# A cross-attention and gated feed-forward layer: queries, keys and values projected turned, their stacks built by way of a scratch in device memory, keys and values by plain fp32 matmuls

## The chip, the core and the metric

The kernel runs on one core of a Trainium2 chip. The metric is the device time of one execution in microseconds (us). One profiled execution of the kernel before is read here; its matrix engine is called PE, its weight loads PEld, the vector engine DVE, the scalar engine ACT, GpSimd POOL and the sync engine SP.

## What is computed

```python
x = x + tanh(g_xattn) * xattn(layernorm(x), ctx, ctx)   # x, ctx: 8 batches x 128 tokens x 512
x = x + tanh(g_ffn)   * ffn(layernorm(x))
# xattn: Q = q Wq + bq (32 heads of 16), K = c Wk + bk, V = c Wv + bv (8 heads of 16, 4 query heads share one)
#        w = softmax(Q K^T / 4); y = w V; return y Wo + bo
# ffn:   h = silu(x w1^T) * (x w3^T); return h w2^T     (512 -> 1792 -> 512; weights come scaled per 128x128 block)
```

All of it is float32, and the result has to be near float32.

## The kernel before, in words

**Products.** A product of near float32 accuracy is made of three fast matmuls in a reduced float32 format (fp32r) on a high and a low part of each side: high by high, high by low, low by high. `three` (lines 1765 to 1769) issues them; line 1767 is the first, 1768 the second, 1769 the third. The high part is a rounding copy on ACT (names ending in `H`), the low part a subtraction on DVE or POOL (names ending in `L`).

**Stages.** A batch is 128 tokens. Eight batches go through attention one after another, overlapped by a hand-written order on each engine: every engine has a straight list of calls with semaphore waits, and it takes them strictly in that order. After the last batch, 28 chunks of the feed-forward follow, in a loop that the change leaves alone; a few matmuls of the first chunks (`g_or_u`) stand between those of the last batches.

**One batch of attention.** `normalise` makes the layer norm, `turn4` turns it with four PE transposes, `x_high` and `x_low` split it. `project` (line 1782) gives the queries with tokens on the partitions (12 matmuls of 512 columns) and `add_bias` (line 1791) adds the bias by one more matmul of 512. Keys and values come together from `project_kv` (12 matmuls of 256 columns, on the context and weights that POOL, ACT and DVE have split) and one bias matmul of 256. `q_high`, `q_low`, `k_high`, `k_low` split them into `Qtok` and `Ktok`. Then `stack_k` and `stack_q` (lines 1795 and 1801, transposes at line 1774) turn them, four transposes at a time, and `k_stacked` and `q_stacked` (lines 614 and 618, ACT) copy the result from PSUM into the stacks: `Qst` and a part of `x2HL`, 96 rows each, in which high and low parts lie under each other so that one matmul of 96 rows gives the whole product. `Qst` holds two batches, in turns; four batches of keys have a place.

`scores` (line 1807) makes the scores of a batch in four parts, into one pair of PSUM banks, and `row_max` (line 1141, DVE) reduces each before the next may be written. The negated maxima are split, turned by `turn_max` and copied by `max_rows`; `max_in` on SP then carries them by four transfers of four rows into rows 96 to 99 of `Qst`. `scores_t` (line 1818) computes the scores again, keys on the partitions, with the maximum already subtracted. `exp_full` and `exp_half` (ACT) and `weight_low` (POOL, line 340) make the weights and their low part, `values` (line 1822, lines 1827 and 1828) the sums over the values, then follow the division, the output projection, the residual and the second layer norm.

**What sets the order.** PE takes `scores(n, 0)` only after the stacks of batch n are there. The first batch has nothing in front of it: there PE waits for weights, for splits and for stacks. SP and ACT issue the transfers; each is a queue of its own, and an issue holds its engine's list for about half a microsecond.

Of the kernel before, what the change touches and what calls it, by code (L numbers as in the profile page):

```python
# [19 lines left out]
F32 = mybir.dt.float32  # L20
F32R = mybir.dt.float32r
# [22 lines left out]
TOK = HT * P  # L44
W13 = 2 * KB * P
# [9 lines left out]
KV0, Q0, O0 = 0, KB * 2 * KVD, KB * 2 * KVD + KB * DM  # L55
PW = O0 + KB * DM
QH = Q0 + KB * DM // 2
BQ, BK, BO = 0, DM, DM + 2 * KVD
BIAS1, BIAS = BO, BO + DM
NCT, NKST = 4, 4  # L60
NWARM = 14
GATE, SC = BIAS, BIAS + 2
# [3 lines left out]
def build(nc, x, ctxt, wproj, small, wff, out):  # L66
    with ExitStack() as ctx:
# [22 lines left out]
        ctH, ctL = (context.enter_context(nc.sbuf_tensor(n, [P, 2, DM], F32R)) for n in ("ctH", "ctL"))  # L90
# [27 lines left out]
        ones = sa("ones", [P, P], F32R)  # L118
        neghalf, unit = sa("neghalf", [P, 1]), sa("unit", [P, 1])
        small1 = sa("small1", [P, 32])  # L120

        Qtok = sa("Qtok", [P, PAIRS * GJ, 3, 32], F32R)
        xTH = sa("xTH", [P, DM], F32R)
        xTL = sa("xTL", [P, DM], F32R)
        xn = sa("xn", [P, DM])
        Qst = sa("Qst", [P, 2, PAIRS, GJ * P], F32R)
        Ktok = sa("Ktok", [P, PAIRS, 2, 3, 2, DH], F32R)
        st1, mv1, ve1, rs1, nb1 = (sa(n, [P, w]) for n, w in (("st1", 6), ("mv1", 2), ("ve1", 1), ("rs1", 1), ("nb1", 1)))
        st2, mv2, ve2, rs2, nb2 = (sa(n, [P, w]) for n, w in (("st2", 6), ("mv2", 2), ("ve2", 1), ("rs2", 1), ("nb2", 1)))
        setup = ctx.enter_context(ExitStack())  # L130
        browf = sa("browf", [P, BIAS1], F32, setup)
        sel = sa("sel", [P, 2, P], F32, setup)
        one2 = sa("one2", [P, P], F32, setup)
        setup.close()
        E = sa("E", [P, NE, GJ * P])
        aTL = sa("aTL", [P, DM], F32R)
        x2n = sa("x2n", [P, DM])
        brow = sa("brow", [P, BIAS1], F32R)
        rden = sa("rden", [P, HEADS])
        vres = sa("vres", [P, KVH, DH])  # L140
# [12 lines left out]
        w2L = sb("w2L", [P, 2, DM], F32R)  # L153
        hH = sb("hH", [P, 2, TOK], F32R)
        hL = sb("hL", [P, 2, TOK], F32R)

        wkv_in, wq_in, wq2_in, wo_in, bias_in, gsc_in, bo_in = (
            sem(n) for n in ("wkv_in", "wq_in", "wq2_in", "wo_in", "bias_in", "gsc_in", "bo_in"))
# [3 lines left out]
        consts, zeros, constr, browz, tanhg = (sem(n) for n in ("consts", "zeros", "constr", "browz", "tanhg"))  # L162
        wpH_ok, wpL_ok, browH_ok, brow_ok, woL_ok, tg_ok = (sem(n) for n in ("wpH_ok", "wpL_ok", "browH_ok", "brow_ok", "woL_ok", "tg_ok"))
        sel_in, bo_ok, stats1, mean1, ve1_ok, rs1_ok = (sem(n) for n in ("sel_in", "bo_ok", "stats1", "mean1", "ve1_ok", "rs1_ok"))
        nb1_ok, xn_ok, xT_ps, xTH_ok, xTL_ok, q_ps = (sem(n) for n in ("nb1_ok", "xn_ok", "xT_ps", "xTH_ok", "xTL_ok", "q_ps"))
        qtokH, qtokL, ctH_ok, ctL_ok, kv_ps, ktokH = (sem(n) for n in ("qtokH", "qtokL", "ctH_ok", "ctL_ok", "kv_ps", "ktokH"))
        ktokL, v1_ok, r1_ok, v2_ok, v3_ok, kst_ps = (sem(n) for n in ("ktokL", "v1_ok", "r1_ok", "v2_ok", "v3_ok", "kst_ps"))
        kst_ok, qst_ps, qst_ok, s_ps, max_ok, mH_ok = (sem(n) for n in ("kst_ok", "qst_ps", "qst_ok", "s_ps", "max_ok", "mH_ok"))
        mL_ok, mT_ps, mrows, mrow_in0, mrow_in1, mrow_in2 = (sem(n) for n in ("mL_ok", "mT_ps", "mrows", "mrow_in0", "mrow_in1", "mrow_in2"))
        mrow_in3, st_ps, E_ok, PH_ok, pL_ok, pv_ps = (sem(n) for n in ("mrow_in3", "st_ps", "E_ok", "PH_ok", "pL_ok", "pv_ps"))  # L170
# [3 lines left out]
        scaled, w13H_ok, w13L_ok, g_ps, u_ps, t_ok = (sem(n) for n in ("scaled", "w13H_ok", "w13L_ok", "g_ps", "u_ps", "t_ok"))  # L174
        a_ok, h_ok, hH_ok, w2H_ok, w2L_ok, hL_ok = (sem(n) for n in ("a_ok", "h_ok", "hH_ok", "w2H_ok", "w2L_ok", "hL_ok"))
        y_used = sem("y_used")
# [3 lines left out]

        def kst(n):
            s = (NBATCH - NKST + n % NKST) * P
            return x2HL[:, :, :, s:s + P]
# [14 lines left out]
        def _(sp):  # L198
            def context_in(n):
                sp.dma_start(ct[:, n % NCT, :], ctxt[n]).then_inc(ct_in[n % NCT], 16)  # L200

            def select_rows():
                sp.wait_ge(consts, 11)
                for b in range(NKST):
                    for gg in range(2):
                        sp.dma_start(r32(kst(b)[ROWS:ROWS + 4, gg, :, :]),
                                     sel[ROWS:ROWS + 4, gg, :].unsqueeze(1).broadcast_to([4, KB, P])).then_inc(sel_in, 16)

            def max_in(n, h):
                done = (mrow_in0, mrow_in1, mrow_in2, mrow_in3)[h]  # L210
                sp.dma_start(r32(Qst[ROWS:ROWS + 4, n % 2, h, :]), r32(Mrow[4 * h:4 * h + 4, :])).then_inc(done, 16)

            def weights_in(c):
                sp.dma_start(wres[:, c, :], wff[c]).then_inc(wff_in[c], 16)

# [6 lines left out]
            for b in range(1, NCT):  # L222
                context_in(b)
# [2371 lines left out]
```

## Time and profile before

| what | us |
|---|---|
| median of 3 runs | 391.84 (390.97 to 392.38) |
| the profiled execution | 391.85 |
| its span on the core | 390.1 |
| PE busy | 377.4 (97%) |
| DVE busy | 271.7 (70%) |
| ACT busy | 209.1 (54%) |
| POOL busy | 160.5 (41%) |

What lies between the span and the execution's time is 1.75 us. A matmul's record lasts longer than its share of the engine, since matmuls are pipelined: what one costs is read from the distance between two starts, not from its duration. In the views below "x4" stands for four such instructions put into one line, and "[0.88 <-DVE Qtok L1127]" says how long the engine stood idle before the line and whose work ended that.

### The profile page before, as it was taken

The numbers are of one execution on the slowest core, as the hardware profiler recorded it, in microseconds if no ns is written. First come the engines' busy times: TensorE is split into PE (matmuls) and PEld (weight loads), VectorE is DVE, ScalarE is ACT, GpSimd is POOL, SyncE is SP. The second block draws the span as 40 slices with busy tenths as digits, with TensorE's granted clock in tenths as the row PEclk, the third lists the DMA queues.
The fourth block names the chain that finished last, engine by engine and source line by source line (L and its number), as shares of the span: only waits on it lengthen the run. The fifth ranks groups of instructions, "written<-read, shape, count | busy, mean of one in ns | idle before, by whom it ended". The sixth has DMA issues, their size and how long they took to land.

```text
span 390.1 us, 6293 instructions
## 1 busy us (share of the span) xinstructions
PE 377.4 (97%) x2350; PEld 307.5 (79%) x2350; DVE 271.7 (70%) x452; ACT 209.1 (54%) x367; POOL 160.5 (41%) x135
## 2 busy tenths in 40 slices
PE   7789999999998999999999999999999999999996
PEld 5578888888887677878888888888888888888885
DVE  5978998979998967898776777543954344554334
ACT  4678999998999986552332332332332332332320
POOL 6558889898999785264333443000000000000000
PEclk9999999999999999999999999999999999999999
DMA  8903104100000040295000000000200000000002
GB/s 289 342 14 86 32 2 167 46 40 6 2 6 3 3 166 2 86 416 227 0 0 0 0 0 0 0 0 2 108 0 0 0 0 0 0 0 0 0 0 108
DMA packets 6817, 20.98 MB, mean 54 GB/s; under 512 B 875, under 2 KB 1131, under 8 KB 6668
## 3 DMA queue, kind: packets, MB, share of 16 engines
q1 hardware_dynamic: 6364, 19.92, 14.0%
q10 hardware_dynamic: 432, 0.79, 0.5%
q8 instruction: 13, 0.21, 0.2%
q14 instruction: 8, 0.07, 0.0%
HBM read 18.28 MB, written 2.10 MB: 52 GB/s over the span
## 4 chain that ended last, share of the span: by engine, by line
PE 83%; DVE 9%; DMA 3%; SPq 2%; ACT 1%; issue 1%; POOL 0%; DVEq 0%
PE ps L1767 23%; PE ps L1769 23%; PE ps L1768 22%; PE ps L1819 3%; PE ps L1809 3%; PE ps L1774 3%; DMA gsc<-in_small 3%; DVE MX L1142 2%; PE ps L1827 2%; PE ps L1775 1%; PE ps L1828 1%; DVE x2HL L1172 1%; DVE X L1183 1%; DVE aTL L1153 1%; DMA Qst<-Mrow 1%
## 5 line engine op out<-in xcount | busy, mean ns | idle before, releaser
L1767 PE MATMUL ps<-x2HL,w13H 128*128 128x512 f32 x224 | 89.1, 398 | 0.0
L1769 PE MATMUL ps<-x2HL,w13L 128*128 128x512 f32 x224 | 88.6, 395 | 0.0
L1768 PE MATMUL ps<-x2HL,w13H 128*128 128x512 f32 x224 | 88.4, 395 | 0.0
L340 POOL TENSOR_TENSOR PL<-E,PH 128x512 f16<-128x512 f32 x64 | 74.1, 1174 | 13.2 <-ACT E L609 7.2
L351 POOL TENSOR_TENSOR wres<-wres,gsc 128x1536 f32<-128x1536 f32 x14 | 42.5, 3037 | 44.2 <-DVE hf L1196 44.2
L632 ACT ACTIVATE T<-ps 128x512 f32<-128x512 f32 x28 | 16.7, 597 | 79.0 <-PE ps L1769 79.0
L640 ACT ACTIVATE hH<-hf 128x512 fp32r<-128x512 f32 x28 | 17.7, 632 | 63.5 <-DVE hf L1196 63.5
L1769 PEld LDWEIGHTS ps<-x2HL,w13L 128*128 128x128 f32 x224 | 42.0, 187 | 10.4
L1768 PEld LDWEIGHTS ps<-x2HL,w13H 128*128 128x128 f32 x224 | 42.0, 188 | 9.8
L1189 DVE SCALAR_TENSOR_TENSOR A<-T,ps 128x512 f32<-128x512 f32 x28 | 19.2, 685 | 43.8 <-ACT T L632 43.8
L1767 PEld LDWEIGHTS ps<-x2HL,w13H 128*128 128x128 f32 x224 | 42.0, 188 | 9.5
L1767 PE MATMUL ps<-w2H,hH 128*128 128x512 f32 x112 | 44.3, 396 | 0.6 <-DVE x2HL L1172 0.6
L1205 DVE TENSOR_TENSOR hL<-hf,hH 128x512 fp32r<-128x512 f32 x28 | 43.2, 1541 | 2.5
L1769 PE MATMUL ps<-w2H,hL 128*128 128x512 f32 x112 | 43.8, 391 | 0.0
L1768 PE MATMUL ps<-w2L,hH 128*128 128x512 f32 x112 | 43.5, 389 | 0.0
L1142 DVE TENSOR_REDUCE MX<-ps 128x8 f32<-128x1024 f32 x32 | 38.9, 1215 | 4.6 <-PE ps L1809 4.6
L1196 DVE SCALAR_TENSOR_TENSOR hf<-A,ps 128x512 f32<-128x512 f32 x28 | 19.2, 687 | 32.5 <-PE ps L1769 32.2
L609 ACT ACTIVATE E<-ps 128x512 f32<-128x512 f32 x64 | 38.2, 612 | 1.8 <-PE ps L1819 1.6
L1177 DVE TENSOR_TENSOR w13L<-wres,w13H 128x1024 fp32r<-128x1024 f32 x28 | 34.1, 1219 | 5.1 <-ACT w13H L627 5.1
L612 ACT ACTIVATE PH<-ps 128x512 f16<-128x512 f32 x64 | 37.1, 606 | 1.0 <-PE ps L1819 0.6
L627 ACT ACTIVATE w13H<-wres 128x1024 fp32r (+1 forms) x28 | 29.3, 1045 | 0.0
L1819 PE MATMUL ps<-Qst,x2HL 100*128 100x512 f32 x64 | 27.3, 439 | 0.1
(112 smaller groups left out, 712.8 us busy)
## 6 DMA issues: line engine op xcount, KB each, us to landing
wres<-in_wff SPq DMA_DIRECT2D x14, 768.0 KB, 6.7
X<-in_x SPq DMA_DIRECT2D x8, 256.0 KB, 11.1
ct<-in_ctxt SPq DMA_DIRECT2D x7, 256.0 KB, 3.2
raw<-in_wproj SPq DMA_DIRECT2D x3, 512.0 KB, 6.3
out<-X SPq DMA_DIRECT2D x6, 256.0 KB, 2.0
raw<-in_wproj SPq DMA_DIRECT2D x1, 1024.0 KB, 9.4
Qst<-Mrow SPq DMA_DIRECT2D x32, 8.0 KB
out<-X ACTq DMA_DIRECT2D x2, 256.0 KB, 2.1
```

The source lines that it names most:

```text
L340: pool.tensor_tensor(PL[:, g % NL, :], E[:, g % NE, :], PH[:, g, :], ALU.subtract).then_inc(pL_ok, 1)
L351: pool.tensor_tensor(w, w, v, ALU.mult).then_inc(scaled, 1)
L609: act.activation(E[:, g % NE, :], ps[:, g % 2, :], ACT.Exp, scale=SCALE).then_inc(E_ok, 1)
L612: act.activation(PH[:, g, :], ps[:, g % 2, :], ACT.Exp, scale=SCALE).then_inc(PH_ok, 1)
L627: act.activation(w13H[:, s, :], wres[:, n, 0:W13], ACT.Copy).then_inc(w13H_ok, 1)
L1142: dve.tensor_reduce(MX[:, :, h, :], ps[:, 2:4, :].rearrange("p b (j g k) -> p (b j) g k", j=2, g=2), AX.X, ALU.max).then_inc(max_ok, 1)
L1177: dve.tensor_tensor(w13L[:, s, :], wres[:, n, 0:W13], r32(w13H[:, s, :]), ALU.subtract).then_inc(w13L_ok, 1)
L1205: dve.tensor_tensor(hL[:, s, :], hf[:, s, :], r32(hH[:, s, :]), ALU.subtract).then_inc(hL_ok, 1)
L1767: pe.matmul(out_ap, aH, bH, start=start, stop=False)
L1768: pe.matmul(out_ap, aH, bL, start=False, stop=False)
L1769: return pe.matmul(out_ap, aL, bH, start=False, stop=stop)
L1819: pe.matmul(ps[:, g % 2, :], kst(n)[0:ROWS + 4, g % 2, g // 2, :], Qst[0:ROWS + 4, n % 2, g // 2, :], start=True, stop=True).then_inc(st_p ...
```

## The change

The projections come out turned, so that no transpose stands behind them, and they take two batches at a time (256 columns). For queries the weights are the stationary side: `project_q` makes one of four groups of 128 output features for two batches by 12 fp32r matmuls of 256 columns. Keys and values come from `project_kv32`: four matmuls of 256 columns each for two batches, in plain fp32, straight from the context and weights as loaded; the splitting of both goes away. The bias is now per partition and is added by the copies that split, `q_high`, `k_high`, `v_bias`, some of them on DVE. Values have to be turned back (`turn_v`, one transpose a batch).

The stacks are filled by transfers. `queries_out` and `keys_out` write the high and the low part into `qscr` and `kscr` in device memory, `queries_in` and `keys_in` read them back into the rows of the stacks in the layout that the scores need. For the queries' high part one transfer fills 64 rows of `Qst` out of 32 rows of the scratch, read twice, by a source whose first dimension is a repetition of 2. Batch 0 has smaller transfers of its own (`queries_part`). The four rows of maxima for each pair of key heads become 16 rows for all pairs, carried by one transfer (two for batch 0).

The scores go by group of query heads instead of by pair of key heads; the four parts of batch 0 alternate between two pairs of banks. All lists of all engines are in a new order. Among the rest: the query weights' low parts move from DVE to POOL, 16 warm-up matmuls instead of 14, a first exponential ahead of everything on ACT, loads in another order and partly on ACT, `X[6]` among them.

```diff
+        qscr = nc.dram_tensor("qscr", [NBATCH // 2, 2, 2, P, GJ * P], F32).ap()
+        kscr = nc.dram_tensor("kscr", [NBATCH // 2, 2, P, 2, TWO], F32).ap()
...
+        def keys_in(eng, p, t):
+            s = (NBATCH - NKST + 2 * p % NKST) * P
+            eng.dma_start(r32(kall(32 * t, 32 * t + 32)[:, :, s:s + TWO]),
+                         kscr[p, t % 2].rearrange("(r h) g n -> r (h g) n", h=PAIRS)).then_inc((k_in0, k_in1)[p % 2], 16)
+
+        def queries_out(eng, p, low, j0, j1, done):
+            eng.dma_start(qscr[p, low, :, :, j0 * P:j1 * P].rearrange("b r n -> r b n"),
+                         r32((QTL if low else QTH)[:, :, j0:j1, :]).rearrange("r b j q -> r b (j q)")).then_inc(done, 16)
+
+        def queries_in(eng, n, low, done):
+            src = qscr[n // 2, low, n % 2].rearrange("(r h) n -> r (h n)", h=PAIRS)
+            if low:
+                eng.dma_start(r32(Qst[64:96, n % 2, :, :]).rearrange("r h n -> r (h n)"), src).then_inc(done, 16)
+            else:
+                eng.dma_start(r32(Qst[0:64, n % 2, :, :]).rearrange("r h n -> r (h n)"),
+                             src.unsqueeze(0).broadcast_to([2, 32, PAIRS * GJ * P])).then_inc(done, 16)
...
 # SP, for batch 3 (batches 2 and 4 to 7 alike)
+            sp.wait_ge(st_ps, 16)
+            queries_in(sp, 3, 0, q_in1)
...
 # PE
-            def stack_q(h, bank):
-                for j in range(GJ):
-                    m = turn(bank[0:ROWS, j * P:(j + 1) * P],
-                             Qtok[:, h * GJ + j, :, :].rearrange("p t d -> p (t d)"))
-                m.then_inc(qst_ps, 1)
+            def project_kv32(bank, n, w0, k0, k1):
...
+                for k in range(k0, k1):
+                    m = pe.matmul(bank[:, 0:TWO], raw[:, w0 + k * KVD:w0 + (k + 1) * KVD],
+                                  ct[:, n % NCT:n % NCT + 2, k * P:(k + 1) * P], start=k == 0, stop=k == KB - 1)
+                return m
+
+            def project_q(bank, j, k0, k1):
+                for k in range(k0, k1):
+                    c = Q0 + (j // 2) * KB * TWO + k * TWO + (j % 2) * P
+                    w = slice(c, c + P)
+                    m = three(bank[:, 0:TWO], WpH[:, w], WpL[:, w], xTH[:, k, :, :], xTL[:, k, :, :], k == 0, k == KB - 1)
+                return m
...
 # PE, between the last scores_t of batch 1 and the first scores of batch 3
             scores_t(1, 7)
             turn4(W1, ON).then_inc(aT_ps, 1)
             project_q(W2, 3, 2, 4).then_inc(q_ps, 1)
             values(1, 2)
             values(1, 3)
             turn_max(W0, 0, 4)
             project(W1, DM, aTH, aTL, O0, 0)
             turn4(W0, xn).then_inc(xT_ps, 1)
+            pe.wait_ge(q_in1, 64)
             scores(3, 0)
```

## Rows read from the trace of the kernel before

**Rows 1.** The page, busy time by engine, its share of the span, instructions.

```profile
PE 377.4 (97%) x2350; PEld 307.5 (79%) x2350; DVE 271.7 (70%) x452; ACT 209.1 (54%) x367; POOL 160.5 (41%) x135
```

**Rows 2.** Stretches: us, then PE, PEld, DVE, ACT, POOL busy, clock, DMA share, GB/s.

```profile
7.50:33.10 25.60, 20.87 (x154) 17.47 (x154) 20.94 (x41) 17.68 (x30) 13.67 (x11) 1.00 0.51 176
33.10:164.20 131.10, 128.95 (x1230) 106.98 (x1228) 114.48 (x261) 116.44 (x229) 105.82 (x94) 1.00 0.13 41
164.20:384.80 220.60, 219.99 (x950) 177.53 (x949) 129.88 (x141) 71.93 (x108) 34.70 (x12) 1.00 0.09 36
```

**Rows 3.** The same view, the stretch in which the loads run.

```profile
10.00:15.00 5.00, 4.02 (x20) 3.21 (x20) 4.79 (x10) 2.10 (x4) 0.75 (x2) 1.00 1.04 384
```

**Rows 4.** PE in order of time: start us, duration us, line, operation, count.

```profile
1.80 5.59 PE L1863 MATMUL ps<-Ktok 128*128 128x512 f32 x14 [1.80 <-DVE Ktok L1073]
7.47 0.63 PE L1775 MATMUL ps<-ident,xn 128*128 128x128 f32 x4
...
8.87 0.28 PE L1769 MATMUL ps<-WpH,ctL 128*128 128x256 f32 x1
8.99 0.28 PE L1767 MATMUL ps<-WpH,ctH 128*128 128x256 f32 x1
...
11.32 0.40 PE L1768 MATMUL ps<-WpL,xTH 128*128 128x512 f32 x1
11.55 0.39 PE L1769 MATMUL ps<-WpH,xTL 128*128 128x512 f32 x1
...
30.62 0.41 PE L1774 MATMUL ps<-identr,Ktok 128*96 128x128 f32 x4
30.87 0.45 PE L1774 MATMUL ps<-identr,Qtok 128*96 128x128 f32 x4
...
33.08 0.47 PE L1819 MATMUL ps<-Qst,x2HL 100*128 100x512 f32 x1
```

**Rows 5.** The same view, a stretch in the middle of attention.

```profile
50.03 0.63 PE L1775 MATMUL ps<-ident,xn 128*128 128x128 f32 x4
50.41 0.48 PE L1819 MATMUL ps<-Qst,x2HL 100*128 100x512 f32 x1
50.73 0.20 PE L1827 MATMUL ps<-Vp,PH 128*128 128x49 bf16 x1
...
51.25 0.72 PE L1809 MATMUL ps<-x2HL,Qst 96*128 96x256 f32 x4
```

**Rows 6.** Groups by line: busy us, mean ns, idle us before and who ended it.

```profile
L1774 PE MATMUL ps<-identr,Qtok 128*96 128x128 f32 x128 | 13.7, 233 | 1.6 <-DVE Qtok L1127 1.2 <-ACT x2HL L615 0.3
L1774 PE MATMUL ps<-identr,Ktok 128*96 128x128 f32 x64 | 6.9, 231 | 0.3 <-DVE Ktok L1107 0.3
L1793 PE MATMUL ps<-brow,ones 128*128 128x512 f32 x8 | 3.2, 395 | 0.0
L619 ACT ACTIVATE Qst<-ps 96x512 fp32r<-96x512 f32 x32 | 18.7, 598 | 0.9 <-PE ps L1774 0.7
L1142 DVE TENSOR_REDUCE MX<-ps 128x8 f32<-128x1024 f32 x32 | 38.9, 1215 | 4.6 <-PE ps L1809 4.6
```

**Rows 7.** Landing by kind in windows 46 to 50 and 75 to 90, and the page.

```profile
ct<-in_ctxt SPq DMA_DIRECT2D x1, 256.0 KB, 2.6
...
wres<-in_wff SPq DMA_DIRECT2D x1, 768.0 KB, 4.5
...
out<-X SPq DMA_DIRECT2D x6, 256.0 KB, 2.0
```

**Rows 8.** Queue: packets, MB, share; windows 88 to 104, 384 to 390.1, 62 to 70.

```profile
q1 hardware_dynamic: 32, 0.03, 0.7%
...
q1 hardware_dynamic: 288, 0.52, 23.2%
...
q1 hardware_dynamic: 273, 1.44, 44.0%
```

**Rows 9.** SP's issue of the maxima's transfers: ns min, median, max.

```profile
L211 SPq DMA_DIRECT2D Qst<-Mrow x32: 577/577/639, 30.2 to 137.5; - x32
```

More of the change, by code:

```diff
@@ L44 @@
 TOK = HT * P
+TWO = 2 * P
+NM = 4 * PAIRS
 W13 = 2 * KB * P
@@ L166, in build @@
[L166 to L169, printed above, removed]
@@ L198, in _ @@
         def _(sp):
[L199 to L211, printed above, removed]
@@ new lines, in _ @@
+            sp.wait_ge(sel_ok, 3)
+            select_rows(sp, 2)
+            tokens_in(sp, 4)
+            select_rows(sp, 3)
+            out_weights_in(sp)
+            sp.wait_ge(k_ps, 1)
+            context_in(sp, 4)
+            context_in(sp, 5)
+            tokens_in(sp, 5)
+            tokens_in(sp, 7)
+            sp.wait_ge(kT_L, 2)
+            keys_out(sp, 0, 1)
+            sp.wait_ge(kl_out, 16)
+            keys_in(sp, 0, 1)
+            out_bias_in(sp)
+            sp.wait_ge(kT_H_dve, 1)
@@ new lines, in _ @@
+            queries_out(sp, 0, 1, 2, 4, ql_out)
+            context_in(sp, 7)
+            sp.wait_ge(qh_out, 16)
+            queries_part(sp, 0, 0, 2, 4, q_in0)
+            sp.wait_ge(kT_H_dve, 2)
+            keys_out(sp, 2, 0)
+            keys_in(sp, 1, 1)
+            queries_in(sp, 1, 0, q_in1)
+            sp.wait_ge(kT_L, 6)
+            keys_out(sp, 2, 1)
+            sp.wait_ge(mrows, 1)
+            max_in(sp, 0, 0, 2)
+            sp.wait_ge(mrows, 2)
+            max_in(sp, 0, 2, 4)
@@ L1303, in _ @@
+            row_max(1, 3)
+            epsilon(6)
+            dve.wait_ge(xn_ok, 6)
+            mean(7)
+            dve.wait_ge(max_ok, 8)
+            max_high(0, 4)
+            x_low(4, W1)
             dve.wait_ge(pv_ps, 2)
@@ L1811, in scores, with turn_max @@
+            def scores(n, j):
+                b = 0 if n == 0 and j % 2 else 2
+                for h in range(PAIRS):
+                    m = pe.matmul(ps[:, b + h // 2, (h % 2) * TWO:(h % 2 + 1) * TWO],
+                                  Qst[0:ROWS, n % 2, h, j * P:(j + 1) * P], kst(n)[0:ROWS, 2 * h:2 * h + 2, :],
+                                  start=True, stop=True)
                 m.then_inc(s_ps, 1)
-            def turn_max(k, bank):
-                for j in range(GJ):
-                    m = turn(bank[0:4 * PAIRS, j * P:(j + 1) * P], Mtok[:, j, :, :, :].rearrange("p h g t -> p (h g t)"))
+            def turn_max(bank, j0, j1):
+                for j in range(j0, j1):
+                    m = turn(bank[0:NM, j * P:(j + 1) * P], Mtok[:, j, :, :, :].rearrange("p h g t -> p (h g t)"))
@@ L1965, in _ @@
+            pe.wait_ge(v3_ok, 3)
+            turn4(W1, xn).then_inc(xT_ps, 1)
+            pe.wait_ge(max_ok, 7)
+            scores(1, 3)
+            pe.wait_ge(PH_ok, 3)
+            scores_t(0, 4)
+            pe.wait_ge(E_ok, 4)
+            scores_t(0, 5)
+            pe.wait_ge(qT_L, 7)
+            project_kv32(W0, 6, V0, 0, 2)
             pe.wait_ge(pL_ok, 2)
             values(0, 1)
-            pe.wait_ge(ktokL, 6)
+            project_kv32(W0, 6, V0, 2, 4).then_inc(v_ps, 1)
+            pe.wait_ge(mL_ok, 3)
@@ L1979, in _ @@
+            scores_t(0, 7)
+            pe.wait_ge(vT_ok_dve, 1)
+            turn_v(W0).then_inc(vt_ps, 1)
             pe.wait_ge(on_ok, 1)
@@ new lines, in _ @@
+            pe.wait_ge(mrows, 6)
+            pe.wait_ge(aTL_ok, 3)
+            project(W0, DM, aTH, aTL, O0, 0)
+            project(W0, DM, aTH, aTL, O0, 1)
+            pe.wait_ge(q_in1, 96)
+            scores(5, 0)
+            pe.wait_ge(on_ok, 14)
+            values(3, 4)
+            values(3, 5)
+            pe.wait_ge(x2n_ok, 1)
+            pe.wait_ge(qT_L, 16)
+            turn4(W1, x2n).then_inc(x2T_ps, 1)
+            project(W0, DM, aTH, aTL, O0, 2)
+            pe.wait_ge(E_ok, 31)
```

2523 lines of the change are left out of this document (1188 added, 1335 removed).

## The prediction, made before the result was seen

> **What bounds the kernel now.** I read four things in this order. First the busy times: PE is busy for 377.4 of 390.1 us, DVE for 271.7, ACT for 209.1 [rows 1]. Second the stretches: in the lead-in (7.5 to 33.1) PE is busy for 20.87 of 25.60 us, in the attention stage (33.1 to 164.2) for 128.95 of 131.10, behind it for 219.99 of 220.60, all at the full granted clock, 1.00, the 2.4 GHz level [rows 2]. So PE bounds every stage but the lead-in: work taken off it shortens the time one for one, as long as nobody else becomes late. Third, who could: in the attention stage ACT is busy for 116.44, DVE for 114.48 and POOL for 105.82 of the 131.10 us, 89, 87 and 81% [rows 2]. They follow closely, so a shorter PE stage needs less work there too. Fourth the transfers: in the attention stage they use 0.13 of the queues' time, in the lead-in 0.51, and there 384 GB/s run for a while [rows 2, 3]. The room for a detour by way of device memory is in the attention stage and not in the lead-in.
>
> **Prices of PE work**, as the distance of starts. An fp32r matmul of 256 columns costs 0.12 us (8.87 to 8.99; 0.118 over a run of them), one of 512 costs 0.23 (11.32 to 11.55; 0.232 over a run), four stack transposes 0.25 (30.62 to 30.87) [rows 4], four fp32 transposes 0.38 (50.03 to 50.41), two `values` 0.52 (50.73 to 51.25) [rows 5].
>
> **Removed from PE.** The stacks' transposes, 128 and 64 of them [rows 6], are 48 groups of 0.25: 12.0 us. Eight bias matmuls of 512 and eight of 256: 8 x 0.232 + 8 x 0.118 = 2.8 us. The products for keys and values, 8 x 12 of 256: 11.3 us. Nothing else of these hides: they stand on PE, which is full.
>
> **Changed and added on PE.** Queries: 8 x 12 matmuls of 512 (22.3 us) become 4 x 48 of 256 (22.7): +0.4. Keys and values: 4 x 8 plain fp32 matmuls of 256 columns. The trace has none. The low bound is one fp32r matmul, 0.118, 3.8 us in all; the high bound is four of them and a weight load of 0.188 beside each pair that nothing hides, about 0.66, 21.1 us. I take 4 x 0.118 = 0.47, 15.1 us, because a full product of two values that each need a high and a low part has four partial products, and the kernel now drops the smallest of them. (The Trainium skill, FP8 and Floating Point Precision, TensorE Precision Notes, says that true fp32 takes four passes through the array; no row here shows it, and by it this term stays 15.1.) The price speaks against this part of the change: 15.1 for 11.3 on PE, paid so that POOL, ACT and DVE need not split context and weights. Eight `turn_v` transposes at 0.095 and one more `turn_max`: +1.0. Two more warm-up matmuls lie in front of the first `turn4`, which waits for the layer norm anyway: 0.
>
> Sum on PE: -12.0 - 2.8 - 11.3 + 0.4 + 15.1 + 1.0 = **-9.6 us**, between -20.9 and -3.6 by the bounds of fp32.
>
> **The other engines.** ACT loses 32 copies into `Qst` (18.7 us by their records [rows 6]), 16 into the key stack and the wide `q_high`; it gains narrower ones and some 20 transfer issues of about half a microsecond. DVE loses the split of the weights and of `Ktok` and gets wider, fewer operations on the values; `row_max`, its largest item at 38.9 us [rows 6], stays. POOL loses the context's splits. I count 15 to 20 us less on ACT, about 12 less on DVE, 8 less on POOL. DVE then has about 102 us of work for a stage in which PE has about 111: 92%, more than now. So relief and crowding nearly cancel. The recorded idle of the stage is 2.15 us [rows 2]; I put the gain from fewer waits at 2.0, between 0 and 5.
>
> **The lead-in.** Now: `scores_t(0, 0)` at 33.08, with 4.7 us of PE idle before it [rows 2, 4]. In the new order PE runs further ahead: all keys, three quarters of the values and two and a half groups of the second queries before its `scores_t(0, 0)`, 27.7 us of work instead of 18.5. What can be late: (1) the value weights are fifth in SP's queue; at 384 GB/s [rows 3] the 2.9 MB issued up to them need until about 10, and PE asks at 9: 1 us. (2) The low keys go out on SP behind 6.4 MB of loads, which last until about 18.4, so they land at about 20; ACT's next key copy waits for that, and behind it in ACT's list stands the first `q_high`, for which PE waits: 1.5 us. (3) Queries out and in, 2.0 and 2.6 us of landing [rows 7] and two issues, against two products for keys and values: 1 us. SP's later waits (for `kl_out`, `kT_H`, `qT_L`) hold `keys_in` and `context_in` behind them, which PE needs some microseconds later. That makes about 3.7 us of idle instead of 4.7: **-1.0**, between -3 and +5.
>
> **The queries' transfers in the stage.** Here a wait is added that was not there. `Qst` holds two batches, so SP may issue `queries_in(n, 0)` only after the last `scores_t` of batch n-2, and PE stands at `scores(n, 0)` until it has landed. Between the two PE has, for n = 3: 0.38 + 6 x 0.118 + 0.52 + 0.25 + 3 x 0.232 + 0.38 = 2.9 us; for the six batches 2 to 7 between 2.9 and 3.9, 3.3 on the mean. Everything behind on PE waits, `scores_t` and `values` included, and with them ACT, DVE and POOL. The transfer is 512 KB. 256 KB landed in 2.6 us and 768 KB in 4.5 [rows 7], so 3.6 by the middle if it runs as wide as those, 3.8 with the wait's end: 0.5 too late, six times: **+3.0**, between 0 and 9. SP's issue itself, 0.58 us at most so far [rows 9], is in it. `max_in` lies behind it in SP's list, and is wanted only after `scores(n, 0)`.
>
> **Sum.** -9.6 - 2.0 - 1.0 + 3.0 = -9.6. From the profiled 391.85 (390.1 of span and 1.75 around it; the median of the runs is 391.84): **382.2 us**. This case's own range is 376 to 388.
>
> **Rival A, slower: the transfer of the queries' high part runs on two engines only.** The queue's packets can be counted. Four of the maxima's transfers, four rows each, leave 32 packets: 8 each, four of data and four more. Two outputs of 128 rows leave 288: 144 each, 128 of data and 16 more [rows 8]. The extra packets are one per transfer engine that takes part, so four rows ran on four engines and 128 rows on 16. The new source has a first dimension of 2 (the repetition), its destination 64 rows. The trace has no transfer whose two sides differ, so it leaves open which side decides. If the source does, each of two engines moves 262 KB. In 62 to 70, 1.44 MB took 44% of 16 engines' 8 us, 25.6 GB/s for one [rows 8]: 10.2 us, with the fixed part of about 2.0 (256 KB landed in 2.6, of which 0.65 at full rate) 12.2. Less 3.3 of cover: 8.9, six times, 53. Batch 1 has such a transfer too, with some 4.4 us of cover: 7.8. In place of my +3.0 that gives 382.2 - 3.0 + 61 = 440. And PE, idle for 8.9 us seven times, would come back at the lower clock, 1.2 GHz, if it does after such a gap what it does at the start: there 14 matmuls took 5.59 us [rows 4], 2.3 more than 14 x 0.232. Seven times 2.3: 456. Middle: **448 us**. For it: the exact count of packets. Against it: the same count fits a rule that goes by the rows of SBUF, which are 64, and every transfer of many rows has run on 16.
>
> (The Trainium skill, DMA: Bandwidth & Descriptors, the section on why a DMA increments its semaphore by 16, says that the slowest dimension of both access patterns sets the number, and its checklist names a leading zero-stride broadcast as a trap. By that rule rival A is what happens. The trace agrees with it where both sides are equal, and does not test the case at hand.)
>
> **Rival B, about no change: crowding.** If fp32 costs 0.66, the sum loses 6.0; if the lead-in's round trips cost 5 instead of gaining 1, it loses 6.0 more; if DVE at 92% holds PE up, the 2.0 of relief go. Any two of them: 391 us.
>
> **Rival C, faster: fp32 in one pass**, 11.3 us less: 371 us. Four partial products speak against it.
>
> **Chances.** The forecast 0.55, all of it faster. A 0.33, all slower. B 0.09, a third each way. C 0.03. Faster by over 0.3% (about 1.2 us, what a measurement of this kernel can tell from no change): 0.55 + 0.03 + 0.03 = 0.61; within it 0.03; slower 0.36. To leave out no more than 2 in 10 the range has to take in most of A, so it runs from 375 to 452; C, the tail of A with a clock that always falls, and the edges of the forecast are outside.
>
> **What would show it.** In the profile of the changed kernel: the fp32 group 0.47 apart (0.12 or 0.66 otherwise); `scores_t(0, 0)` at about 39 us; the waits of PE for `Qst` out of `qscr` at about 0.5 each; landing of the 512 KB at 3.6 us and 64 + 16 packets (A: 12 us, 64 + 2, a clock below 1.00 behind each gap); DVE at about 92% in the stage; the stage behind attention unchanged at 220 us. The prediction is wrong if PE's idle time in the attention stage passes 10 us, or if the fp32 group is not near 0.47.

## The result, and the profile of the changed kernel

The changed kernel takes 523.83 us (median of 4 runs, 522.23 to 526.05), the kernel before 392.11 on the same chip: ratio 1.337, 95% interval 1.331 to 1.343. The forecast was 382.2, its range ended at 452, and rival A's middle was 448. One run each of e6_batch5 (443.85), e12_halves (428.35) and, beside e5_split, the kernel before (1286.66) came out slow, and these three are left out of every comparison below.

The page of the changed kernel: span, busy times, the granted clock in 40 slices (tenths of full speed), two queues, and the chain of work that ended last.

```profile
span 524.3 us, 6001 instructions
...
PE 391.3 (75%) x2216; PEld 318.8 (61%) x2216; DVE 269.0 (51%) x440; ACT 181.0 (35%) x309; POOL 150.3 (29%) x126
...
PEclk9885595675876858667599999999999999999999
...
q1 hardware_dynamic: 13454, 30.28, 18.3%
...
PE 57%; DMA 28%; issue 5%; ACT 4%; DVE 2%; SPq 2%; POOL 1%; ACTq 0%; DVEq 0%; POOLq 0%
```

Against [rows 1], PE is idle for 133.0 us instead of 12.7, and it is busy for 13.9 us more though it has less to do: the clock was at full speed everywhere before, and falls to about half in many slices here. Over a quarter of the chain is transfers. Stretches, cut as [rows 2] are (lead-in, attention, what is behind it; us, busy time of PE, PEld, DVE, ACT, POOL, clock, share of the DMA engines, GB/s):

```profile
7.50:66.10 58.60, 37.64 (x185) 32.53 (x185) 26.69 (x57) 15.59 (x28) 17.18 (x14) 0.74 0.61 191
66.10:298.40 232.30, 126.74 (x1067) 103.98 (x1066) 105.45 (x230) 92.39 (x173) 94.61 (x89) 0.74 0.25 69
298.40:519.00 220.60, 219.00 (x945) 176.45 (x944) 130.24 (x140) 71.25 (x106) 33.73 (x11) 1.00 0.08 34
```

The first transposed scores come at 66.1 instead of 33.1 (+33.0), attention lasts 232.3 instead of 131.1 (+101.2), and what is behind it is as long as before. That is the whole difference of the spans, 134.2. What PE waited for (us in total, times, longest):

```profile
PE ps L1878 <- DMA Qst<-qscr: 97.5, 8, 20.0
PE ps L1878 <- DMA x2HL<-kscr: 16.3, 1, 16.3
PE ps L1859 <- DMA ct<-in_ctxt: 4.3, 3, 2.0
PE ps L1832 <- ACT VT L687: 3.1, 1, 3.1
```

Nine waits make 113.8 of the 133.0 us of idle time. One of them in order of time on PE, with two matmuls at the lower clock behind it (start us, duration us; in square brackets the idle time ahead and who ended it):

```profile
142.50 0.50 PE L1889 MATMUL ps<-Qst,x2HL 112*128 112x512 f32 x1 [0.21 <-ACT PH L705]
...
162.11 1.19 PE L1878 MATMUL ps<-x2HL,Qst 96*128 96x256 f32 x4 [16.03 <-DMA Qst<-qscr]
163.10 0.63 PE L1832 MATMUL ps<-WpH,aTH 128*128 128x512 f32 x1
163.53 0.63 PE L1833 MATMUL ps<-WpL,aTH 128*128 128x512 f32 x1
```

The queries of batch 4 were issued at 143.04 and PE went on at 162.11: 19.1 us for 512 KB. For the batches 2 to 7 this time is 19 to 23 us, and PE stood idle for 15 to 20 of them. Behind the gap, matmuls of 512 columns start 0.43 apart, the 1.2 GHz level, where they start 0.23 apart at 2.4 GHz [rows 4]. While that transfer runs nearly alone (146 to 161 us) the queue shows this (packets, MB, share of 16 engines):

```profile
q1 hardware_dynamic: 77, 0.50, 12.7%
```

12.7% of 16 is 2.03 engines. The maxima's and the keys' transfers issued behind it wait too: the maxima of batch 3 (`Qst<-Mrow`, 128 KB) landed after 18.6 us. SyncE itself is held, too. Its list behind the queries of batch 3:

```profile
112.15 1.63 SPq L224 DMA_DIRECT2D qscr<-QTL  x1
113.82 11.43 SPq L220 DMA_DIRECT2D x2HL<-kscr  x2
```

The last two issues have no wait between them in the program and took 11.4 us, where one issue took 0.58 before [rows 9]. At 178.50 the list stands for another reason, a semaphore: SyncE may read the last keys back only after their low part has landed in device memory, and that transfer lies behind the queries of batch 5.

```profile
SPq L220 <- DMA kscr<-KTL: 22.0, 2, 16.1
```

It stood for 16.1 us there, and only then issued the two remaining keys' transfers and the queries' way out of the last pair.

### The profile page after: what moved, and what is told of

The parts are those of the page before. It is cut to its first block, busy times and chain, and to the rows that moved or that the text cites. A ratio compares the mean times of both kernels' runs of the same rounds, so it can differ in the third digit from the quotient of the medians.

```text
span 524.3 us, 6001 instructions
## 1 busy us (share of the span) xinstructions
PE 391.3 (75%) x2216; PEld 318.8 (61%) x2216; DVE 269.0 (51%) x440; ACT 181.0 (35%) x309; POOL 150.3 (29%) x126
## 3 DMA queue, kind: packets, MB, share of 16 engines
q1 hardware_dynamic: 13454, 30.28, 18.3%
## 4 chain that ended last, share of the span: by engine, by line
PE 57%; DMA 28%; issue 5%; ACT 4%; DVE 2%; SPq 2%; POOL 1%; ACTq 0%; DVEq 0%; POOLq 0%
DMA Qst<-qscr 20%; PE ps L1832 16%; PE ps L1834 16%; PE ps L1833 16%; DMA x2HL<-kscr 4%; PE ps L1878 3%; PE ps L1889 2%; DMA kscr<-KTL 2%; DMA X<-in_x 2%; ACT E L702 2%; ACT PH L705 1%; PE ps L1840 1%; DMA qscr<-QTH 1%; PE ps L1897 1%; PE ps L1898 1%
## 5 line engine op out<-in xcount | busy, mean ns | idle before, releaser
L1878 PE MATMUL ps<-x2HL,Qst 96*128 96x256 f32 x128 | 28.2, 357 | 114.6 <-DMA Qst<-qscr 97.5
L1878 PEld LDWEIGHTS ps<-x2HL,Qst 96*128 96x128 f32 x128 | 24.2, 252 | 119.9 <-DMA Qst<-qscr 55.8
L721 ACT ACTIVATE T<-ps 128x512 f32<-128x512 f32 x28 | 16.8, 598 | 78.4 <-PE ps L1834 78.4
## 6 DMA issues: line engine op xcount, KB each, us to landing
wres<-in_wff ACTq DMA_DIRECT2D x3, 768.0 KB, 12.2
```

The source lines that it names most:

```text
L1878: m = pe.matmul(ps[:, b + h // 2, (h % 2) * TWO:(h % 2 + 1) * TWO], Qst[0:ROWS, n % 2, h, j * P:(j + 1) * P], kst(n)[0:ROWS, 2 * h:2 * h + ...
```

## Experiments

Every kernel ran on the same chip as the kernel before (391.3 to 392.3 in those comparisons). Where no number of runs is given, the median is of four. Two other kernels, e1_split and e4_batch5, were empty programs through an error in the edit (2.86 us); they measure nothing and came again as e5_split and e6_batch5. e5 to e8 ran on one chip (the kernel before took 392.3 there), e2, e3 and e9 to e12 on a second (391.3 and 391.7), e13 to e16 on a third (391.5); differences of some 1 us between these groups mean nothing.

### The number in front, or the repetition?

**e2_distinct** keeps 2 in front and takes away the repetition: the two halves of the destination are filled from two different pieces of scratch (rows 32 to 63 then hold the low part, so the scores are not quite the reference's). Two added waits see to it that the low part has been written.

```diff
+                eng.wait_ge(ql_outa, 16)
+                eng.wait_ge(ql_out, 16 * (n // 2 + 1))
...
-                             src.unsqueeze(0).broadcast_to([2, 32, PAIRS * GJ * P])).then_inc(done, 16)
+                             qscr[n // 2, :, n % 2].rearrange("c (r h) n -> c r (h n)", h=PAIRS)).then_inc(done, 16)
```

> The changed kernel, but the source of the 64 rows is the high part and the low part of the same batch, two different pieces of the scratch, as a first dimension of 2 and a second of 32; nothing is read twice. The second 32 rows then hold the low part, so the scores are not the layer's. Theory 1 (the number 2 in front decides): 66 packets with two of them at the end, landing still 17 to 22 us, time 515 to 535. Theory 3 (reading the same addresses twice at the same time is what is slow): landing falls to about 12 us, the time to 440 to 470.

Measured: 519.8 us (one run), the waits for `Qst<-qscr` 94.1 us, and as many packets on the queue as in the changed kernel, 13454. So the repetition isn't it.

**e3_rows64** gives source and destination 64 rows in one dimension. The rows are the wrong ones, so that the scores are not the reference's; the amount and the order of the work are.

```diff
-                             src.unsqueeze(0).broadcast_to([2, 32, PAIRS * GJ * P])).then_inc(done, 16)
+                             qscr[n // 2, 0].rearrange("b (r h) n -> (b r) (h n)", h=PAIRS)).then_inc(done, 16)
```

> The changed kernel, but the 64 rows come from 64 rows of the scratch that follow each other (the high part of both batches of the pair) in one dimension; 512 KB in one transfer, as before. The rows are not those that the layer needs. Theory 1: 16 engines, landing 3.5 to 4.5 us, time 376 to 390, like e1_split. Theory 2 (device memory, or so many bytes into so few rows): landing above 10 us, time above 480.

Measured: 425.4 us (one run). The 512 KB land in 4.7 us at the median. The same bytes into the same 64 rows of SBUF, with 64 in front of the source instead of 2, take a quarter of the 19 to 23 us. Together with e2_distinct this leaves the number in front of the source; whether the destination's 64 rows are carried as 64 or as 2 by 32 in the transfer with 2 in front, no run shows.

**e5_split** cuts the transfer in two, with 32 rows in front each, and computes the reference's values.

```diff
-                eng.dma_start(r32(Qst[0:64, n % 2, :, :]).rearrange("r h n -> r (h n)"),
-                             src.unsqueeze(0).broadcast_to([2, 32, PAIRS * GJ * P])).then_inc(done, 16)
+                for t in range(2):
+                    eng.dma_start(r32(Qst[32 * t:32 * t + 32, n % 2, :, :]).rearrange("r h n -> r (h n)"), src).then_inc(done, 16)
...
-            pe.wait_ge(q_in1, 32)
+            pe.wait_ge(q_in1, 48)
...
```

The other six waits of PE for queries are raised in the same way, as each batch now ends with one landing more.

> The changed kernel with one edit: the 512 KB transfer that fills rows 0 to 63 of the stack of queries (2 in front, nothing in the source moved on) is two transfers of 256 KB with 32 rows in front, for all seven batches. The output is the reference's. Theory A, the number in front sets how many engines carry a transfer, and that is where the time went: the landing falls from 19 to 23 us to 4 to 6, and the time comes close to that of the run with 64 rows in one dimension (425.4 us), plus one more issue of 0.5 us in front of each batch: 420 to 432. Theory B, it is the way through device memory that is slow, however the transfer is cut: 500 to 525. My recorded forecast for the changed kernel with a short transfer, 382, is taken as already refuted by the run with 64 rows; what stays of its difference of some 43 us is in the lead-in and in the short waits for queries, at a lower clock, if theory A is right.

Measured: 425.31 us (422.49 to 427.10), ratio to before 1.084 (1.077 to 1.091). 98.5 us of the loss are gone with this one edit. Its landings (KB each, median us), and its queue:

```profile
Qst<-qscr SPq DMA_DIRECT2D x15, 256.0 KB, 4.2
...
q1 hardware_dynamic: 13664, 30.28, 22.8%
```

The packets settle the count on which rival A stood [rows 8]. Seven transfers with 2 in front, at 64 rows and one more packet for each engine, would leave 7 x (64 + 2) = 462; the split ones leave 7 x 2 x (32 + 16) = 672, 210 more. 13664 less 13454 is 210. The next run, with one of the seven as before, has 13634, 30 less. With 64 in front it should be 7 x (64 + 16), 98 more than in the changed kernel, and that trace has 13552: 98 more. (The Trainium skill, DMA: Bandwidth & Descriptors, the section on why a DMA increments its semaphore by 16, has the rule that the slowest dimension of both access patterns sets the number of engines. The trace agrees: with 64 rows of SBUF to fill and 2 in front of the source, the packets are 64 + 2.)

**e6_batch5** leaves the old transfer in batch 5 alone.

> As the split kernel, but batch 5 alone keeps its single transfer with 2 in front. Theory A: one landing of 19 to 23 us instead of 4 to 6, so about 14 to 17 us idle in one place, and lower clock after it for a few us: the split kernel plus 14 to 21. If the loss had needed all seven together (a queue that never drains), one alone would cost under 8.

Measured: 437.11 us (one run), 11.8 above the split kernel, between the two ranges expected. PE in its trace:

```profile
134.14 1.22 PE L1881 MATMUL ps<-x2HL,Qst 96*128 96x256 f32 x4 [16.33 <-DMA Qst<-qscr]
```

The waits for queries rose from 16.8 to 29.7 us in all, 12.9 more, and attention by 11.4 (155.2 against 143.8). So one such transfer costs nearly what it adds to PE's waits. Seven times 11.8 is 83, against 98.5 measured, so most of the loss comes from each transfer by itself. With one run here, and four of the split kernel that spread over 4.6 us, it is not shown that the missing 16 us are real; if they are, the held issues and the wait for keys of the changed kernel are where to look.

### What the lower clock costs

**e7_fill** is the changed kernel with fillers in front of six of the waits.

```diff
+            def fill(count):
+                for i in range(count):
+                    pe.matmul(ps[:, 2, :], identr[:], WpH[:, Q0:Q0 + DM], start=True, stop=True)
...
+            fill(64)
             pe.wait_ge(q_in1, 64)
             scores(3, 0)
```

> The changed kernel, its transfers as they are, with 64 matmuls of 512 columns that nobody reads ahead of TensorE's wait for the queries of each of the batches 2 to 7, where it stood about 16 us each time. At 0.23 us each they last 14.8 us and end inside the wait. Theory C, the idle stretches bring the clock down to 0.5 and what runs behind them pays: some 16 of the 23.5 us that I put down to the clock come back, 500 to 512 us. Theory D, the clock is low for another reason or its price is smaller than worked out: 518 to 527. If the fillers themselves run at the low clock (0.43 each, 27 us) they end behind the landing, and the time rises to over 550.

Measured: 522.2 us (521.2 and 523.1) against 523.8 (522.2 to 526.1), so the runs can't be told apart; it lies in the range of theory D. The mean clock rose from 0.857 to 0.950, and the waits for `Qst<-qscr` fell from 97.5 to 27.1 us. PE's attention stage in the profiled run:

```profile
67.80:293.60 225.80, 208.54 (x1450) 171.29 (x1450) 104.82 (x229) 92.05 (x173) 94.68 (x89) 0.95 0.26 71
```

It is 6.5 us shorter than the 232.3 of the changed kernel; the start was 1.7 us later. The stage is a ring: the queries of a batch are issued after the last transposed scores of the batch two before, and PE goes on when they have landed. In the changed kernel one turn takes 30.5 and 33.1 us (issues at 143.04, 173.53 and 206.59), of which 19.1 and 20.8 pass until PE goes on; the remaining 11.4 and 12.2 are work of PE and ACT. Over the five turns of the batches 2 to 6 this remainder is 57.3 us, and 51.2 with the fillers. So of the 23 us by which PE's records are longer than its work (391.3 against 368.1, worked out below), these two profiles give back about 6, and the medians 1.7; the profiled run of the changed kernel is the slowest of its four, the one with fillers the faster of its two. The fillers did not lift the clock everywhere: the four scores behind the gap of batch 3 took 1.22 us with them too, against 0.72 behind the next. The time from the issue until PE goes on hardly changed, 123.5 us for the six batches and 122.7 with the fillers.

**e11_fill** puts fewer fillers into the split kernel: 12 for each of the batches 2 to 7, 12 ahead of the second projection of queries and 18 ahead of the first scores.

> The split kernel with matmuls of 512 columns that nobody reads in front of TensorE's longer waits: 12 ahead of the second projection of queries (it stood 3.4 us there), 18 ahead of the first scores (4.1 us), 12 ahead of the queries of each of the batches 2 to 7 (2 to 4 us). In the changed kernel such fillers lifted the mean clock from 0.86 to 0.95 and moved the time by 1.7 us, since there the transfer set the pace. Theory C, in the split kernel TensorE is the bound between its short waits, so its low clock (0.78 to 0.91 in 60 to 160 us, 0.956 over all) is paid: 414 to 421 us. Theory D, what sets the pace there too is the ring of queries, maxima and exponentials: 423 to 428.

Measured: 416.13 us (415.68 to 416.53), 9.2 less than the split kernel. Attention in the split kernel and in this one:

```profile
54.40:198.20 143.80, 122.77 (x1067) 100.27 (x1066) 105.36 (x230) 92.14 (x173) 95.20 (x90) 0.91 0.41 111
```

```profile
53.60:188.00 134.40, 128.41 (x1139) 104.76 (x1138) 104.67 (x230) 91.96 (x173) 94.64 (x88) 1.00 0.43 119
```

The first of the two is the split kernel's. The second has 72 matmuls more, 16.7 us at 0.232, and is 9.4 us shorter. Here the transfer is over in 4 us, PE sets the pace between its waits, and the clock that its idle time brings down is paid. The expectation (theory C) holds. The lead-in hardly moved (53.6 for 54.4) while its mean clock rose from 0.89 to 0.96, so what sets it is not the clock.

### The waits for the queries in the split kernel

**e12_halves** brings the queries of the batches 2 to 7 in two halves, the first of which is enough to begin.

```diff
+        def queries_halves(eng, n, rows):
+            for j in (0, 2):
+                for t in rows:
+                    queries_part(eng, n, t, j, j + 2, ((q_in0a, q_in1a) if j == 0 else (q_in0, q_in1))[n % 2])
...
-            queries_in(sp, 3, 0, q_in1)
+            queries_halves(sp, 3, (0, 1))
```

> The split kernel, where the queries of the batches 2 to 7 come in two halves, heads 0 and 1 of each group first, in six transfers of 128 KB, and TensorE begins its scores when the first three have landed. If the transfer's landing of 4 to 5 us is what it waits for (16.8 us in seven waits, 12.4 us more than before between the first transposed scores and the last values), about half of each wait goes: 416 to 421 us. If the extra issues on SyncE (four at 0.6 us in place of two) and on ScalarE take it away again, or the ring is paced elsewhere: 424 to 430.

Measured: 423.29 us (three runs, 421.10 to 423.89), which lies between the two ranges expected and can't be told from the split kernel (422.49 to 427.10). The waits did fall by half. In the split kernel, and then in this one:

```profile
PE ps L1878 <- DMA Qst<-qscr: 16.8, 7, 4.1
```

```profile
PE ps L1883 <- DMA Qst<-qscr: 8.8, 5, 3.1
```

The clock of 80 to 100 us rose from 0.83 to 1.00, but those of 40 to 60 and 60 to 80 fell from 0.87 and 0.91 to 0.74 and 0.83, and a wait of 3.0 us for GpSimd came up. So most of the 8 us by which the waits became shorter did not reach the end.

### What sets the start

The chain that ended last, in the start of the split kernel (start us, us, what), its long pieces:

```profile
4.51 9.24 DMA X<-in_x
...
16.38 6.59 DMA kscr<-KTL
23.12 0.47 ACT KTH L683
...
26.75 7.26 DMA qscr<-QTH
...
35.26 3.52 DMA qscr<-QTL
38.80 7.99 DMA Qst<-qscr
```

34.6 of 47 us are landings. 256 KB took 6.6 to 9.2 us, and the last piece, 128 KB of queries, 8.0, where I had reckoned with 2.0 and 2.6 for 256 KB [rows 7]: the queues carry loads at the same time (0.80 of their time in 7.5 to 54.4, against 0.51 in the lead-in before [rows 2]).

**e8_late** loads the output weights (1 MB) and the tokens of batch 7 behind the first queries.

```diff
-            out_weights_in(sp)
...
-            tokens_in(sp, 7)
...
             queries_part(sp, 0, 0, 2, 4, q_in0)
+            out_weights_in(sp)
             sp.wait_ge(kT_H_dve, 2)
...
             queries_in(sp, 1, 0, q_in1)
+            tokens_in(sp, 7)
```

> The split kernel with 1.25 MB less on the queues of the lead-in: the output weights (1 MB) and the tokens of batch 7 are loaded behind the first queries instead of ahead of the first keys. Theory E, the lead-in is slow because keys, queries and their way back land late among the loads (6 to 8 us each where 3 to 4 were reckoned): 1.25 MB at some 390 GB/s is 3.3 us, so the first maxima and everything behind them come 3 to 6 us earlier than in the split kernel. Theory F, the lead-in is a chain of round trips whose length the loads don't set: within 1.5 us of the split kernel. Over 2 us slower if the output weights now hold up ScalarE or GpSimd, which wait for them ahead of the first E.

Measured: 427.28 us (425.75 to 428.39), 2.0 above the split kernel with overlapping runs. The first keys' way out took 3.2 us instead of 6.6 and the first scores came at 34.6 instead of 38.3. But the third keys, now behind the weights, took 6.9 us, and ACT stood for them; the first transposed scores came at 53.9 (54.4).

**e9_late2** puts the weights behind the third keys.

> The split kernel with the output weights (1 MB) and the tokens of batch 7 (256 KB) loaded behind the third keys on their way out, where the kernel that deferred them less far had them in front. There the first scores came 3.7 us earlier (34.6 instead of 38.3), and the third keys, now behind 1 MB, took 6.9 us and gave it all back. Theory E, the lead-in pays for what stands on the queue in front of each transfer of its chain: the 3.7 us stay, 419 to 423 where the split kernel took 425.3. Theory F, the start is set by something else that only shows when the first delay goes: within 1.5 us of it.

Measured: 428.41 us (426.62 to 430.27). In the chain:

```profile
16.61 3.36 DMA kscr<-KTL
...
24.36 8.40 DMA qscr<-QTL
...
37.60 10.34 DMA raw<-in_wproj
48.17 1.61 issue
49.78 0.47 ACT VT L687
50.29 0.58 PE ps L1832
```

The keys' way out is short again, but ACT has its copy of the output weights ahead of a copy of the values in its list, so it stands until they have landed, and PE behind it. First transposed scores: 58.8. The expectation of 419 to 423 is wrong, for want of reading ACT's list.

**e10_order** also loads the tokens of batch 2 and the value weights ahead of the query weights.

> As the run before it (output weights and tokens 7 late), and the tokens of batch 2 and the value weights loaded ahead of the 2 MB of query weights. In the split kernel the chain of waits begins with the landing of those tokens, 9.2 us at 4.5 to 13.8, because VectorE takes their statistics ahead of the low part of the first keys. Theory E: they land some 3 us earlier, the query weights later by less than GpSimd can spare; another 1 to 3 us less than the run before, 416 to 422. If the query weights set the pace (GpSimd splits them for 4.7 us from 10.8 on, and TensorE wants them at 24) it gives them back: the same as the run before or up to 3 us more.

Measured: 426.99 us (425.80 to 429.59), not the 416 to 422 of theory E. The tokens left the chain and the context took their place (`ct<-in_ctxt` landed after 10.1 us); the wait for the output weights stayed on it. In this start a new order of the loads only changed who was late.

**e13_shift** is e9_late2 with ACT's copy of the output weights moved to the end of batch 0, and GpSimd's low part behind it.

```diff
-            weights_high(wo_in, O0, PW, woH_ok)
             v_bias(W0)
...
             queries_in(act, 2, 1, q_in0)
+            weights_high(wo_in, O0, PW, woH_ok)
```

> The split kernel with the output weights loaded behind the third keys as before, and the work on them (ScalarE's copy to the high part, GpSimd's low part) moved from ahead of the first maxima to the end of batch 0. In the two kernels that only moved the load, ScalarE stood 4.6 to 4.9 us at 43 to 48 and held up a copy of values that TensorE wanted. Theory E (crowded queue): with that wait gone the 3 to 4 us by which the first scores came earlier are kept, first transposed scores at 48 to 51 instead of 54.4, 419 to 423. Theory G (ScalarE's waits for the keys' and queries' way out set the start): 424 to 428.

Measured: 422.06 us (418.40 to 424.58), first transposed scores at 53.3. 6.4 us less than e9_late2 came back with ACT's wait; against the split kernel it is 3.2, and the runs overlap. The time lies in the range of theory E, but its sign, first transposed scores at 48 to 51, did not come: the profiled run doesn't bear it out.

**e15_keys2** is the split kernel with a second buffer for the keys of the second pair, so that ACT needn't wait until the first pair has left.

```diff
-            act.wait_ge(kh_out, 16)
-            act.wait_ge(kl_out, 16)
-            k_high(W0, 0)
+            k_high(W0, 0, 1)
...
-            act.wait_ge(kh_out, 32)
-            act.wait_ge(kl_out, 32)
+            act.wait_ge(kl_out, 16)
```

> The split kernel with buffers of their own for the keys of the second pair of batches, so that ScalarE's copy of them no longer waits until the first pair has left for device memory (4.9 us in which the copy of the queries and the values stood behind it), and the copy of the third pair waits for the first pair alone (5.6 to 6.8 us before). Theory G: the queries leave some 4 us earlier, first transposed scores at 49 to 51, 418 to 422. Theory E: what leaves earlier waits on the crowded queue instead: 423 to 427.

Measured: 423.26 us (421.73 to 424.07). The first transposed scores came at 49.8 instead of 54.4, as theory G had it, but at most 2.1 us of these 4.6 reached the end, as theory E had it, and 0.7 of them lie between the chips. PE waits for queries 18.9 us in six times, against 16.8 in seven.

**e16_all** has e13_shift, e15_keys2 and the fillers of e11_fill.

> The last two together with the fillers in front of TensorE's long waits (which took the split kernel from 425.3 to 416.1). Theories E and G together: first transposed scores at 45 to 49, and 405 to 411; if the fillers' gain and these are the same microseconds, 412 to 416. I expect no version with the ring through device memory to come under the kernel before (391.7) with these means: the ring's sum of landings ahead of the first scores (34 us of 47 in the split kernel) stays over 20.

Measured: 415.06 us (413.27 to 418.16), mean clock 1.00. First transposed scores at 49.9. Against e11_fill (416.13) it is the same within the runs: as the expectation had it for the case that the gains are the same microseconds. Its stretches, at full clock:

```profile
7.50:49.90 42.40, 36.28 (x218) 31.30 (x217) 26.77 (x60) 14.21 (x27) 12.81 (x13) 1.00 0.90 267
49.90:185.90 136.00, 128.86 (x1140) 105.04 (x1139) 104.94 (x232) 93.90 (x175) 99.42 (x90) 1.00 0.43 118
```

The DMA engines are busy 0.90 of the start. No version came under the kernel before.

## Why the prediction was wrong, step by step

**The sum on PE: right.** e16_all shows PE's work at full clock, with 102 fillers in it:

```profile
PE 391.8 (95%) x2318; PEld 318.5 (77%) x2318; DVE 268.6 (65%) x441; ACT 180.6 (44%) x309; POOL 150.5 (37%) x126
```

391.8 less 102 x 0.232 is 368.1, 9.3 us under [rows 1]; the sum said 9.6. One term in it was 1.3 too dear (the next paragraph), and what took that back was not traced. In attention 128.86 less 72 x 0.232 is 112.2, and I had written about 111.

**The price of fp32: right within a tenth.** Each fp32 matmul stands in the trace as two instructions (64 records for 32 matmuls). Eight records, four matmuls, in the changed kernel, and what starts behind them:

```profile
31.50 1.89 PE L1859 MATMUL ps<-ct,raw 128*128 128x256 f32 x8
33.23 0.60 PE L1840 MATMUL ps<-ident,xn 128*128 128x128 f32 x4
```

By the distance of the starts, 1.73 us, that is 0.43 for one and 13.8 us for 32, where I had taken 0.47 and 15.1. Rival C, one pass, is out. (By the Trainium skill, FP8 and Floating Point Precision, TensorE Precision Notes, true fp32 takes four passes; the trace agrees, 0.43 being 3.7 times 0.118.)

**The choice between the forecast and rival A: this is the step that failed.** The term of +3.0 for the queries' transfers let 512 KB land in 3.6 us, "if it runs as wide as those" of the rows; it ran on two engines, landed in 19 to 23, and made PE wait 97.5 us. I gave 0.33 to the rival in which the number in front of the source decides and 0.55 to the one in which the 64 rows of the destination do. I had two packet counts in which both sides were equal and left the case open, with the larger chance for the pleasant side. e2_distinct and e3_rows64 show that 2 in front of the source is enough, with 64 rows to fill. Its worth: 98.5 us, by e5_split.

**The size of rival A: too small.** It said 12.2 us of landing and 8.9 of waiting, 448 with half the price of the clock. Measured: 19 to 23 us, and 15 to 20 of waiting, 17 on the mean. The term that was mis-sized is the rate of one engine, 25.6 GB/s, taken from a stretch of other transfers [rows 8]. In 146 to 161 us two engines move 33 GB/s, 16.5 each, and 262 KB take 16 us at that. In the split kernel, in 134 to 139.5 us, two queues move 1.1 MB in 83% of 16 engines' time, 15 each: it is the pace in these stretches, not of two engines only. Why it is lower than 25.6 no run tells. And the rival had counted nothing for others: keys and maxima behind it on the queue, two issues of SyncE that took 11.4 us (1.6 for the same two in the split kernel), its wait of 16.1 us for keys.

**The clock: right that it falls; its cost in the changed kernel is not settled.** The rival put 16 us on it, and e7_fill gives back 1.7 by the medians and 6.5 in the attention stage of the profiled runs, with the clock still low behind some gaps. In the split kernel it costs 9, and there I had reckoned with none.

**What stays of the difference in the split kernel, 425.3 against 382.2.** By its stretches:

- The start: first transposed scores at 54.4, where I had reckoned 39: +15.4. The step "what can be late" added 3.7 us of idle time from three transfers at 2.0 to 2.6 us. There are five landings on the chain, 34.6 us. Rival B's 5 for the lead-in's round trips, 6 more than the forecast, was too small as well. I had seen the loads (6.4 MB until about 18) and ended them there; in 20 to 40 us they still took 0.83 of the queues in this kernel. That ACT's copy of the keys waits for the way out, and the queries behind it, I had, at 1.5 us; it stood 5.0, and twice 5.2 more for what went out later. What moved the start was e15_keys2 (4.6 us), while orders of loading alone gave nothing that the runs can tell.
- Attention: 143.8 us. I expected 131.1 less 9.6 less the 6 by which the start was to be late, 115.5. The remaining 28.3 are 21.0 of PE idle (143.8 less 122.8; I had 3 for the queries and hardly anything besides), some 17.5 too many, and 10.6 of lower clock (122.8 less 112.2). The queries' transfer landed in 4.2 instead of 3.6, so the size of the transfer was nearly right, but PE waited 16.8 us in seven times, 2.4 each instead of 0.5.

15.4 and 28.3 make 43.7, with 382.2: 425.9. That agrees with 425.3. How much of the idle time of attention comes from the late start, through which queries and keys of the next pairs collide with it, I can't say: e15_keys2 made the start 4.6 us earlier and the end at most 2.1.

**Behind attention: right.** 219.0 us of PE in 220.6, unchanged.

**Relief of the other engines: right in direction, of no use.** DVE 105.45 us of attention, ACT 92.39, POOL 94.61 in the changed kernel against 114.48, 116.44 and 105.82 before [rows 2]. PE waited 3.1 us for ACT's copy of the values and 118.1 for transfers of queries, keys and context, and at most 1.6 for any other engine's work. DVE at 92% of a stage of 111 us never came to be tested.

## What to carry to other kernels

Before a copy on an engine is exchanged for a detour through device memory, write down for each transfer its first dimension on both sides, how often it stands on the chain, and what it finds on the queue at that time; a landing of 2.6 us on an idle queue was 6 to 9 in this start. If the one measured row leaves two readings of a rule open, and one of them costs 60 us, forecast by the dearer or have the edit written so that the question doesn't arise: two transfers of 32 rows took 0.8 us to issue here, one 0.5, and they saved 98.

Ask of a low clock what it costs before paying for a high one: fillers in front of the waits gave back 9 us in the split kernel, where TensorE is the bound between short waits, and 1.7 by the medians (6.5 in the attention stage of the profiled run) where each wait is for a transfer of 19 us or more.

Before an issue is called slow, read each one's own duration and the waits between them. The view of SyncE's list has one line for the three issues from 178.50 on in the changed kernel:

```profile
178.50 17.91 SPq L220 DMA_DIRECT2D x2HL<-kscr  x3
```

The first of them took 0.56 us and the other two together 1.21; the rest of the 17.9 is the wait for the keys.

## What the runs showed of the hardware that I had not expected

- What was issued on the same queue behind a transfer on two engines waited for it: 128 KB of maxima landed after 18.6 us at the median (5.0 in the split kernel), and two issues of SyncE took 11.4 us, against this in the split kernel:

```profile
87.16 1.60 SPq L220 DMA_DIRECT2D x2HL<-kscr  x2
```

- One DMA engine made 15 to 16.5 GB/s in the stretches with the queries' transfers, with two engines at work and with 13 of 16 alike, against 25.6 in a stretch of the kernel before.
- A plain fp32 matmul of 256 columns is two instructions in the trace, 0.216 us apart (1.73 us for eight).
- 72 useless matmuls made the split kernel's attention 9.4 us shorter: the mean granted clock of the stage was 1.00 with them and 0.91 without.
